# One power for the statistics of three batches, and one region of the packed buffer for each expert

## What is computed

```
logits = x @ router_w.T ; scores = sigmoid(logits) ; s = scores + bias        # 16 experts, 4 groups
group_score = top_k(s by group, 2).sum ; keep the 2 best groups ; topk_idx = top_k(masked, 4)
tw = scores[topk_idx] / (sum + 1e-20) * 2.5
routed = sum over e of tw_e * (silu(x @ gate_e) * (x @ up_e)) @ down_e ; out = routed + shared(x)
```

## Time and profile before

| What | Value |
|---|---|
| Median of 3 runs | 1013.03 us (1012.64 to 1014.21) |
| The profiled execution: its time | 1015.96 us |
| The profiled execution: its span | 1014.1 us |
| Mean granted PE clock in it | 0.938 |
| PE busy | 883.9 us (87%) |
| DVE busy | 579.2 us (57%) |
| ACT busy | 438.1 us (43%) |
| POOL busy | 432.5 us (43%) |

### The profile page before, as it was taken

One profiled execution on the slowest core, in us unless ns is written; L12 is line 12 of the kernel. 1 busy time (PEld: TensorE's weight loads), 2 busy tenths in 40 slices (PEclk: granted clock), 3 DMA queues, 4 the chain that ended last, 5 costly groups with the idle time before them and its releaser, 6 DMA issues.

```text
span 1014.1 us, 19554 instructions
## 1 busy us (share of the span) xinstructions
PE 883.9 (87%) x5726; PEld 633.2 (62%) x5727; DVE 579.2 (57%) x1675; ACT 438.1 (43%) x1167; POOL 432.5 (43%) x603
## 2 busy tenths in 40 slices
PE   5888799677779999999999955899699999999970
PEld 2555599555658888888888743456455555555540
DVE  2889758664248999878777767722123333333325
ACT  1444355334137777767676731122122223322223
POOL 3799512103054555332322200377534455544453
PEclk9999899796879999999999977899899999999995
DMA  6620011997010000003232103163425555554547
GB/s 222 203 69 21 11 37 43 292 134 103 20 46 1 3 2 2 7 13 110 74 111 74 38 1 124 55 231 132 158 46 88 88 87 86 86 86 85 89 62 253
DMA packets 71788, 85.99 MB, mean 85 GB/s; under 512 B 18208, under 2 KB 63136, under 8 KB 71200
## 3 DMA queue, kind: packets, MB, share of 16 engines
q1 hardware_dynamic: 56544, 63.05, 24.3%
q0 software_dynamic: 14448, 19.34, 10.6%
q10 hardware_dynamic: 720, 2.63, 0.7%
HBM read 48.76 MB, written 36.97 MB: 85 GB/s over the span
## 4 chain that ended last, share of the span: by engine, by line
PE 68%; POOL 10%; DVE 10%; issue 5%; DMA 4%; ACT 2%; POOLq 0%; SPq 0%; DVEq 0%; ACTq 0%
PE bank L913 42%; PE bank L926 7%; POOL grid L868 6%; PE bank L1273 6%; PE bank L1259 3%; PE bank L1283 3%; DMA inT<-in_xT 2%; PE bank L1254 1%; POOL arena L787 1%; DMA const<-in_const 1%; DVE arena L2049 1%; DMA ys<-arena 1%; PE bank L1068 1%; POOL arena L782 1%; PE bank L905 1%
## 5 line engine op out<-in xcount | busy, mean ns | idle before, releaser
L913 PE MATMUL bank<-arena 128*128 (+7 forms) x1312 | 418.1, 459 | 17.7 <-ACT arena L1443 9.4
L913 PEld LDWEIGHTS bank<-arena 128*128 128x128 f32 (+1 forms) x1312 | 232.7, 197 | 122.7 <-issue 86.6
L878 POOL DMA_INDIRECT ys<-arena x79 | 122.6, 1552 | 137.3 <-DVE arena L2173 126.2
L926 PEld LDWEIGHTS bank<-const,arena 128*128 128x128 f32 x636 | 77.8, 142 | 89.4 <-issue 73.9
L926 PE MATMUL bank<-const,arena 128*128 128x128 f32 x636 | 104.3, 279 | 20.1 <-DVE arena L2062 10.3
L2165 DVE SCALAR_TENSOR_TENSOR arena<-arena,bank 128x256 f32<-128x256 f32 x79 | 38.0, 480 | 146.7 <-ACT arena L1637 146.7
L765 POOL TENSOR_TENSOR lr<-mv,const 128x1 f32<-128x1 f32 x64 | 12.1, 188 | 243.1 <-DVE mv L1681 243.1
L2049 DVE TENSOR_REDUCE arena<-bank 128x4 f32<-128x512 f32 x128 | 86.7, 677 | 38.4 <-PE bank L1259 38.4
L1637 ACT ACTIVATE arena<-bank 128x256 f32<-128x256 f32 x79 | 30.3, 383 | 174.6 <-PE bank L913 174.6
L913 PE MATMUL bank<-arena,inT 128*128 128x256 f32 (+1 forms) x256 | 86.1, 464 | 18.9 <-DMA inT<-in_xT 10.2
L1587 ACT ACTIVATE arena<-arena 128x512 f32<-128x512 f32 x128 | 81.1, 633 | 34.8 <-DVE arena L2052 34.4
(11 more groups left out here) (266 smaller groups left out, 1337.8 us busy)
## 6 DMA issues: line engine op xcount, KB each, us to landing
arena<-in_f_w SPq DMA_DIRECT2D x18, 768.0 KB, 4.7
arena<-grid SPq DMA_DIRECT2D x79, 137.0 KB, 2.2
grid<-arena SPq DMA_DIRECT2D x1, 10112.0 KB, 43.9
inT<-in_ctxT SPq DMA_DIRECT2D x32, 128.0 KB, 2.1
arena<-ys SPq DMA_DIRECT2D x8, 512.0 KB, 6.8
inT<-in_xT SPq DMA_DIRECT2D x16, 128.0 KB, 2.1
X<-in_x SPq DMA_DIRECT2D x1, 2048.0 KB, 8.4
arena<-in_c_w SPq DMA_DIRECT2D x2, 1024.0 KB, 6.5
```

What stands on the lines that cost most here:

```text
L878: pool.indirect_dma_start(ys, bass.IndirectOffsetOnAxis(ap=number, axis=0), s_y[t.ring(YR)], None, compute_op=ALU.add).then_inc(l_sy[t.rin ...
L913: m = pe.matmul(o, lhs[k], rhs[k], start=k == 0, stop=k == n - 1)
L926: m = pe.transpose(o[:, k * width:(k + 1) * width], src(k), ident[0:width, 0:width])
```

## The change

**One power.** `a_rms_`, `a_orms_` and `ln_power(A_)` become one POOL step. `a_var` holds five values: the mean, the variance of batch t-6, the output's mean square of batch t-4, and the two of q and k of batch t. `a_power_(t)` adds the epsilons to four of them, takes one power of 128x4, and makes -mean times root. The final step moves from DVE to ACT (`a_final_`, lag 8, at the head of ACT's list). The lags of `a_y_`, `a_sum_`, `ln_bn` go from 5 to 6, that of `ln_aggr` from 6 to 7. POOL runs `a_power_` six times more after the last batch.

**A region for each expert.** `grid` grows from 79 to 272 tiles: 16 tiles for each expert, then 16 for unused slots. A token's row needs only its expert and its place within the expert, so batches 0 to 7 get their rows before batches 8 to 15 are routed. Each slot's tile number is computed (`f_src`), and SP loads it into a register before each load of a tile. The fill writes whole rows of 274 values to 272 tiles, after the other fills have landed. The routing of the first half is spread over batches 9 to 15 of stage E; that of the second half over `shared(0)` to `shared(4)`.

```diff
+NTILE = E * TMAX + E
+    c[:, SPARSE["region"]] = TMAX * P * e
-        ROUTED_AFTER = 1
+        ROUTED_AFTER = (0, 4)
-            sp.dma_start(grid.rearrange("(a p) w -> p a w", p=P)[:, :, 0:D],
-                          f_fill.unsqueeze(1).to_broadcast([P, NSLOT, D])).then_inc(l_fill, 16)
-            sp.dma_start(grid[:, D:XW], a["spare"]).then_inc(l_fill, 16)
+            sp.dma_start(f_fill[:, D + E:XW], a["spare"]).then_inc(l_fill, 16)
...
+            sp.wait_ge(l_fill, 16 * 3)
+            sp.dma_start(grid.rearrange("(a p) w -> p a w", p=P),
+                          f_fill.unsqueeze(1).to_broadcast([P, NTILE, XW])).then_inc(l_fill, 16)
-                if b == 2:
-                    sp.wait_ge(f_routed, 2)
+                if b == 4:
+                    sp.wait_ge(f_routed, 4)
                     for e in range(4, 7):
                         sp.dma_start(W[:, e, :], a["f_w"][e]).then_inc(l_w[1], 16)
-                sp.dma_start(s_x[t.ring(SR)], grid[t.b * P:(t.b + 1) * P, :]).then_inc(l_sx[t.ring(SR)], 16)
+                tile = sp.value_load(f_src[0:1, t.b:t.b + 1], min_val=0, max_val=NTILE - 1)
+                sp.dma_start(s_x[t.ring(SR)], grid_tiles[:, bass.ds(tile, 1), :].rearrange("p a w -> p (a w)"))\
+                    .then_inc(l_sx[t.ring(SR)], 16)
...
+            def a_power_(t):
+                if not t.peeled or t.b < B:
+                    wait(pool, a_sq, t, 2)
+                    wait(pool, a_relu, t, 2, back=2)
+                else:
+                    wait_end(pool, a_relu)
+                if not t.peeled or t.b < B + 4:
+                    wait(pool, a_osq, t, 1, back=4)
+                    wait(pool, a_y, t, 1, back=6)
+                else:
+                    wait_end(pool, a_y)
+                wait(pool, stats, t, 2, back=6)
+                wait(pool, normed, t, 1, back=8)
+                if t.peeled and t.b == 0:
+                    pool.wait_ge(a_ready, 1)
+                pool.tensor_tensor(a_var[t.p][:, 1:5], a_var[t.p][:, 1:5], eps, ALU.add).then_inc(a_pow.sem, 1)
+                wait(pool, a_pow, t, 1)
+                pool.tensor_tensor(a_pw[t.p][:, 1:5], a_var[t.p][:, 1:5], c("half"), ALU.pow).then_inc(a_pow.sem, 1)
+                wait(pool, a_pow, t, 2)
+                hold(pool)
+                pool.tensor_scalar(a_pw[t.p][:, 0:1], a_var[t.p][:, 0:1], a_pw[t.p][:, 1:2], -1.0,
+                                   ALU.mult, ALU.mult).then_inc(a_pow.sem, 1)
-            pipelined(pool, [(ln_power(A_), 6), (a_orms_, 5), (a_swap_, 1), (a_turn_, 1), (a_rms_, 1)])
+            pipelined(pool, [(a_swap_, 1), (a_turn_, 1), (a_power_, 1)], peel=10)
+            for b in range(B, B + 6):
+                a_power_(turn(b))
-            pool.wait_ge(f_routed, 2)
             for b in range(B):
+                if b % HB == 0:
+                    pool.wait_ge(f_routed, 2 + 2 * (b // HB))
...
+            def a_final_(t):
+                wait(act, a_pow, t, 3, back=-6)
+                act.activation(X[:, t.b, 0:D], y[t.p][:], ACT.Identity, scale=a_pw[t.p][:, 1:2],
+                               bias=a_pw[t.p][:, 0:1]).then_inc(normed.sem, 1)
-            pipelined(act, [(a_osq_, 5), (a_fTc_, 3), (a_sq_, 1), (a_relu_, 2), (a_atc_, 4)])
+            pipelined(act, [(a_final_, 8), (a_osq_, 5), (a_fTc_, 3), (a_sq_, 1), (a_relu_, 2), (a_atc_, 4)])
...
-            pipelined(dve, [(a_ob_, 5), (ln_aggr(A_), 6), (a_div_, 4), (a_kvm_, 3), (ln_final(A_), 6),
-                            (a_rope_, 2), (a_y_, 5), (a_qkb_, 0), (a_sum_, 5), (a_vb_, 1), (ln_bn(A_), 5)])
+            pipelined(dve, [(a_ob_, 5), (ln_aggr(A_), 7), (a_div_, 4), (a_kvm_, 3),
+                            (a_rope_, 2), (a_y_, 6), (a_qkb_, 0), (a_sum_, 6), (a_vb_, 1), (ln_bn(A_), 6)])
...
+            first_half = {9: lambda: f_groups_(0), 10: lambda: f_best_(0), 11: lambda: f_pick_(0, 0),
+                          12: lambda: f_pick_(0, 1), 13: lambda: f_pick_(0, 2), 14: lambda: f_pick_(0, 3),
+                          15: lambda: f_sums_(0)}
...
             dve.wait_ge(l_fc, 32)
+            f_weights_(0)
+            f_places_(0)
+            shared(0)
             f_groups_(1)
-            shared(0)
-            f_picks_(1, (0, 1))
+            f_best_(1)
             shared(1)
-            f_picks_(1, (2, 3))
+            f_pick_(1, 0)
+            f_pick_(1, 1)
+            shared(2)
+            f_pick_(1, 2)
+            f_pick_(1, 3)
+            shared(3)
+            f_sums_(1)
+            f_weights_(1)
+            shared(4)
+            f_places_(1)
+            shared(5)
```

More of the change, by code:

```diff
@@ L331, in build @@
         a_v = [A(KC, VW) for _ in range(2)]
-        a_ms = [A(2) for _ in range(2)]
+        a_var = [A(5) for _ in range(2)]
         a_sqs = [A(3, D) for _ in range(2)]
-        a_r = [A(2) for _ in range(2)]
+        a_pw = [A(5) for _ in range(2)]
         a_u = [A(2 * D) for _ in range(2)]
@@ L506, in build @@
         a_sq = step("a_sq", 2)
-        a_rms = step("a_rms", 2)
+        a_pow = step("a_pow", 3)
+        a_ready = sem("a_ready")
         a_swap = step("a_swap", 2)
@@ L787, in a_turn_ @@
                 pool.tensor_tensor(a_u[t.p], a_qk[t.p], a_cos, ALU.mult).then_inc(a_turn.sem, 1)
[L789 to L801, removed]
@@ L1337, in h_down_, with f_pos_ @@
                     .then_inc(h_dp.sem, 1)
+            def f_pos_(half):
+                flat = lambda v: v.rearrange("p b e -> p (b e)")
+                first, mine = HB * half, slice(HB * half, HB * (half + 1))
+                lower = flat(f_sum[0])[:, E * max(first - 1, 0):E * (first + HB - 1)]
+                pe.wait_ge(l_fc, 32)
+                pe.wait_ge(f_routed, 1 + 2 * half)
+                pe.matmul(bank[0][:, 0:HB * E], fc("tri"), flat(f_sel[:, mine]), start=True, stop=False)
+                m = pe.matmul(bank[0][:, E * (half == 0):HB * E], fc("ones"), lower, start=False, stop=True)
+                if half == 1:
+                    m = pe.matmul(bank[0][:, HB * E:(HB + 1) * E], fc("ones"), f_sum[0][:, B - 1, :], start=True, stop=True)
+                m.then_inc(f_pos, 1)
             pe.wait_ge(l_w[0], 16 * 11)
@@ L1677, in stage @@
                 def stage(t):
-                    wait(dve, rstd.again(round), t, 1, back=2)
+                    if round == A_:
+                        wait(dve, a_pow, t, 3, back=-4)
+                    else:
+                        wait(dve, rstd.again(round - 1), t, 1, back=2)
                     wait(dve, st, t, 1)
                     hold(dve)
-                    dve.bn_aggr(mv[t.p][:], bn[t.p][:]).then_inc(st.sem, 1)
+                    dve.bn_aggr(a_var[t.p][:, 0:2] if round == A_ else mv[t.p][:], bn[t.p][:]).then_inc(st.sem, 1)
                 return stage
@@ L1686, in stage @@
                 def stage(t):
[L1687 removed]
+                    wait(dve, rstd.again(round - 1), t, 2)
                     o = X[:, t.b, 0:D] if to is None else to(t)
@@ L1695, in _ @@
                 dve.memset(a_v[i][:, :, P:VW], 1.0)
+            for i in range(2):
+                m = dve.memset(a_var[i], 1.0)
+            m.then_inc(a_ready, 1)
             dve.wait_ge(l_const, 16)
@@ L1761, in a_y_ @@
             def a_y_(t):
-                wait(dve, a_orms, t, 2)
+                wait(dve, a_pow, t, 2, back=-4)
                 wait(dve, normed, t, 1, back=2)
-                dve.scalar_tensor_tensor(out=y[t.p][:], in0=a_o[t.p], scalar=a_or[t.p][:, 1:2], in1=row("gout"),
+                dve.scalar_tensor_tensor(out=y[t.p][:], in0=a_o[t.p], scalar=a_pw[t.p][:, 2:3], in1=row("gout"),
                                          op0=ALU.mult, op1=ALU.mult).then_inc(a_y.sem, 1)
@@ L1982, in f_groups_, with f_best_ @@
                 route(dve.tensor_reduce(gs, f_pair, AX.X, ALU.max))
+            def f_best_(half):
                 one = f_gs.unsqueeze(2).to_broadcast([P, HB, GROUPS, GROUPS])
@@ new lines, in f_pick_, with f_sums_ @@
+                route(dve.tensor_tensor(eq, key, over_e, ALU.is_equal))
+                if n == 0:
+                    dve.tensor_copy(f_sel[:, at], eq)
+                else:
+                    dve.tensor_tensor(f_sel[:, at], f_sel[:, at], eq, ALU.add)
+                route(dve.scalar_tensor_tensor(out=flat(f_v), in0=flat(eq), scalar=-BIG, in1=flat(f_v),
+                                               op0=ALU.mult, op1=ALU.add))
+            def f_sums_(half):
+                at = slice(HB * half, HB * (half + 1))
+                shift = [f_sel[:, at], f_sum[0][:, at], f_sum[1][:, at], f_sum[0][:, at]]
+                for n in range(3):
+                    d, old, new = 1 << n, shift[n], shift[n + 1]
+                    dve.tensor_copy(new[:, 0:d, :], old[:, 0:d, :])
+                    route(dve.tensor_tensor(new[:, d:HB, :], old[:, d:HB, :], old[:, 0:HB - d, :], ALU.add))
+                if half == 1:
+                    route(dve.tensor_tensor(shift[3], shift[3], f_sum[0][:, HB - 1:HB, :].to_broadcast([P, HB, E]), ALU.add))
```

(18 more changed lines are left out.)

135 lines of the change are left out of this document (54 added, 81 removed).

## The result

The changed kernel takes 1000.13 us (median of 4 runs, 998.89 to 1002.29); the kernel before took 1013.61 beside it. The ratio is 0.987, with a 95% interval from 0.9848 to 0.9892. The forecast was 1000.1, the range 994 to 1007.

The account below looks back on a forecast made before the run. The prediction took POOL, then DVE, to pace the last half of stage A, and PE to wait on routing and scatters around the shared experts. From span 1014.1, -15.0 + 2.1 = -12.9 gave 1001.2, median 1000.1, range 994 to 1007.

Parts of the forecast that it names:

- A, steady part: Stage A's repeating period falls from 5.98 to 5.35 us, saving 4.4 us in seven periods.
- POOL's 5.0: In stage A, POOL's work per period falls from 5.98 to 5.0 us.
- DVE's 5.2: In stage A, DVE gives up the final step and its wait, 0.75 us, going from 5.98 to 5.2 a period.
- A, the end: Where A meets B, ACT's longer queue brings `copy_xT` 5.0 us later (bounds 4 and 6.5).
- the term of 1.5: At B's start, first products at half rate after PE's pause cost 1.5 us (bounds 0 and 4).
- Fill: The 38.2 MB grid fill takes about 162 us, ends near 350, and costs 0.
- The rival of 1065: The fill runs at 129 GB/s, `e_w` lands at 489, E starts 65 us late: median about 1065, chance 0.05.
- Routing in E: Spread routing costs E +1.2 us (0.5 to 3), the tail saves 5.0: batch 15's final step 3.8 earlier.
- Shared experts: From E's tail through the shared experts: earlier scatters and fewer waits bring the first slot's transpose to 717.1 from 732.08, -15.0 us.
- The scatters take over: Rival in the shared experts: scatters slow to 1.25 + 0.3 us beside DVE, first slot near 728, median 1011; chance 0.08.
- The sum: Whole kernel: -15.0 + 2.1 = -12.9 us, span 1001.2, median 1000.1.
- the end of A costs more: Rival in stage A: DVE sets the pace, the 4.4 is lost, stage 8 us slower, median 1006; chance 0.14.

Follow-up runs that it names:

- final_on_dve: The changed kernel with stage A's last step on VectorE as in the kernel before, not on ScalarE: 997.72 us, ratio 0.9831 to the kernel before.
- after: The changed kernel itself, as measured and profiled after the change, against the kernel before: 1000.13 us, ratio 0.987.
- power_alone: The kernel before with only the edits of stage A (one power, last step on ScalarE): ratio 0.9996 to the kernel before.
- late_finals: The changed kernel with A's last two steps on ScalarE put behind B's first two transposed-tile copies and first copy of the queries: 996.23 us, ratio 0.9839.
- fill_alone: The kernel before with only the large fill of 272 tiles, slots still reading the first 79: ratio 0.9979 to the kernel before.
- late_half: The changed kernel with the first half's routing put back to batches 13 to 15 of E: E and tail 3.2 us more than the change, 4.0 in the median.
- region_alone: The kernel before with all edits outside stage A: median 1004.67 us, ratio 0.9873 to the kernel before.
- late_scatter: The changed kernel with GpSimd waiting for both halves' places before its first scatter: 1025.82 us, ratio 1.0094 to the kernel before.
- after_again: The changed kernel unaltered, measured again beside the other kernels: ratio 0.9866 to the kernel before.
- early_b: The changed kernel with ScalarE's last two steps of A put behind its first two copies of B's transposed tiles: ratio 0.9936 to the kernel before.

## Why the prediction was right, term by term

- **A, steady part.** Period 5.40 for 5.35, 4.1 us in seven for 4.4. That POOL's 5.0 was near is luck. Its three small operations take 1.71 a period (13.7 us in eight), where the working gives 1.41 (2.40 - 1.5 + 0.31 + 0.2), and its three large ones take 2.97 for 3.55, which I did not foresee. DVE's 5.2 was wrong in what it rests on: final_on_dve shows that the step cost almost nothing there.
- **A, the end.** From the last read of `a_osq_` to `copy_xT` 2.9 us became 8.8: +5.9 for +5.0, within 4 to 6.5. The last step takes 0.60 on ACT, not the 0.41 that I carried over from DVE, and the last `a_y_` waits 1.59 for it. The half rate was there, 124 to 130, and B's part from `copy_xT` on grew by 1.9 (49.86 to 51.77) for 1.5. The prediction gave for the start at 0.50, but their windows show 0.82 and 0.80; the trace of the kernel before has it from 596.6 to 600, behind the wait of 6.05. What I did not count is A's first eight batches, 2.8 us earlier. The net at B's end was +1.2 and +1.9 in the two traces of after and -1.1 in power_alone, for +2.1.
- **The half rate alone.** late_finals without the long pause keeps 1.00 from 120 to B's end and needs 50.5 us from the same copy to there, 1.3 less than the change. So the term of 1.5 stood at about 1.3. The rule of the Trainium skill that the prediction named (TensorE: Matmul & The Clock Gate, "Why this matters for your kernels"), no pauses between bursts, agrees with both traces.
- **Fill.** 134.8 us for 162, no cost seen (fill_alone). The rival of 1065 is dead: the rate was 283 GB/s, not 129.
- **Routing in E.** E +0.73 for +1.2, the tail -3.9 for -5.0; together -3.2 for -3.8, and late_half returns all of it.
- **Shared experts.** Counted from D's end, to take the clock of C out: the second product starts at 166.0, predicted 165.9; the last `h_y_` is 0.5 later than predicted, the first slot's transpose 1.1 later. -13.85 stands for -15.0. The last step, 4.33 for 3.7, is half of the difference; its parts in the prediction (0.4, 0.3 to 0.5, 2.1 after 713.8) add up to 716.6 to 716.8, not to 717.1. At the lower clock of region_alone the phase is 2.6 longer, so the nearness of this term, too, is partly the clock's.
- **The scatters take over.** 81.6 us from first to last for 80.0; one takes up to 1642 ns, the median is 961, and a slack of 7 hides the 1.6. The Trainium skill (DMA: Bandwidth & Descriptors, "SWDGE vs HWDGE vs iDMA") has GpSimd locked out by some DVE instructions while it writes descriptors. Whether the 1.6 is that is not shown: late_scatter, whose scatters start after all places are made, still has one of 1497 and takes 80.9.
- **The sum.** after_again: +1.9 +0.7 (clock) -1.5 (D, clock) +0.7 -3.9 -10.5 +0.1, 12.5 at the first load of `ys`, for -12.9.

The mechanism was right: the region gains, the power with the last step on ACT does not. That the size was met to 0.1 us is luck, as errors cancel: the region gained 1 less, the start of A 2.8 more, the end of A cost 1 more, and the clock moves a single trace by more than each of these. The rival "the end of A costs more" was not far off in kind: this end is the place where some 4 us more were to be had.

## What to carry to other kernels

Count what stands behind an operation in its new engine's queue before its price: a step of 0.6 us on an engine that was busy less than half of the time cost 4 to 5 us, because the next stage's first copies stood behind it and TensorE then came back at half rate. If a result can be placed without knowing the total (a region for each expert), the transfers can start with the first half of the input. Without that nothing of this gain is left (late_scatter); spreading the first half's routing over seven batches is worth 3 to 4 us of it (late_half). Where TensorE pauses often, one profile each can't price an edit of a few us: compare the stages it touches, and take the whole from many runs.

## What was not expected of the hardware

- One transfer of 38.2 MB ran at 283 GB/s where the old one of 10.4 MB had 236, and fill_alone shows no loss beside it; but a transfer of 1 MB that was queued 88.9 us into it took 45.3 us, to 0.6 before its end.
- In stage A, another of DVE's operations is now the slow one beside POOL: `a_y_` went from 1075 to 472 ns, the rotation's sum from 682 to 901. DVE's groups from 62 to 105 us, two of the kernel before, then two of after:

```profile
L1764 DVE SCALAR_TENSOR_TENSOR y<-arena,rows 128x256 f32<-128x256 f32 x8 | 8.6, 1075 | 0.0
L1729 DVE TENSOR_TENSOR arena<-arena 128x512 f32<-128x512 f32 x8 | 5.5, 682 | 0.0
...
L1765 DVE TENSOR_TENSOR arena<-arena 128x512 f32<-128x512 f32 x8 | 7.2, 901 | 0.0
L1800 DVE SCALAR_TENSOR_TENSOR y<-arena,rows 128x256 f32<-128x256 f32 x8 | 3.8, 472 | 0.0
```

  POOL's swap went from 0.95 to 1.28 us down to 0.84. The Trainium skill (GPSIMD Engine Reference, "1. Specifications") has the two engines contend for SBUF when DVE reads two inputs from it; both operations do. The edit of stage A brings it, as power_alone has the same durations (473, 873 and 845 ns) and region_alone the old ones (1078, 681, 1074). That contention is the cause is not shown, nor which part of the edit, the merging or the new lags, does it; the rotation's sum is back at 681 once the last step is on DVE.
- TensorE kept full rate over pauses of 1.34 and 0.51 us (late_finals), and was at half rate after one of 1.34 followed by one of 2.98 (early_b) and after one of 6.66.
- The same 428 matmuls of C took 97 to 104.7 us, at a mean granted clock of 0.86 down to 0.76.
